# A causal triangular solve with tokens on partitions: 32 tokens in two steps, no transposes between them

## The reference, cut to what matters

```
probs = softmax(q k^T * scale + causal_mask)          # 512 x 512 per head
L     = eye - tril(probs, -1)
rhs   = diagonal(probs)[:, None] * v
A     = solve_triangular(L, rhs, lower=True)          # each token needs all earlier ones
x     = x + A @ Wd.T + bd
```

## Time and profile before

| | |
|---|---|
| median of 3 runs | 1506.54 us (1501.0 to 1509.91) |
| profiled execution, span | 1507.1 us (0.6 us over the median) |
| the layer of the change | about 628 to 1181 us; its 16 solves 719 to 1181 us |
| PE busy | 1237.4 us (82%), 11642 matmuls |
| PEld busy | 673.8 us (45%), 11642 weight loads |
| DVE / ACT / POOL busy | 1035.0 / 729.2 / 628.0 us |
| instruction blocks fetched by DMA queue q8 | 92, 1.51 MB |

### The profile page before, as it was taken

One profiled execution on the slowest core, in us unless ns is written; L12 is line 12 of the kernel. 1 busy time (PEld: TensorE's weight loads), 2 busy tenths in 40 slices (PEclk: granted clock), 3 DMA queues, 4 the chain that ended last, 5 costly groups with the idle time before them and its releaser, 6 DMA issues. The chain is left out here.

```text
span 1507.1 us, 30851 instructions
## 1 busy us (share of the span) xinstructions
PE 1237.4 (82%) x11642; PEld 673.8 (45%) x11642; DVE 1035.0 (69%) x2290; ACT 729.2 (48%) x1596; POOL 628.0 (42%) x838
## 2 busy tenths in 40 slices
PE   6656677779999988538889988988988799999976
PEld 2212232222333337424666766666666333333276
DVE  6699999979888955457446646645632588988653
ACT  3834334317766675313524523533442166676754
POOL 2279888853424215314423423223332524351244
PEclk9878888869999998758889879978997599999988
DMA  5378833023224022441421231141120231331213
GB/s 166 145 274 320 298 139 140 20 67 87 55 65 122 13 82 63 100 86 23 88 38 25 45 74 28 21 100 18 18 51 10 67 79 31 97 89 45 81 48 88
DMA packets 137737, 128.41 MB, mean 85 GB/s; under 512 B 92007, under 2 KB 123559, under 8 KB 132202
## 3 DMA queue, kind: packets, MB, share of 16 engines
q1 hardware_dynamic: 129536, 118.56, 28.6%
q0 software_dynamic: 2496, 5.13, 1.1%
q10 hardware_dynamic: 5558, 2.76, 0.9%
HBM read 105.61 MB, written 38.62 MB: 96 GB/s over the span
## 5 line engine op out<-in xcount | busy, mean ns | idle before, releaser
L1393 DVE TENSOR_REDUCE f_row_min<-f_ps 128x1 f32<-128x512 f32 x512 | 323.9, 676 | 55.6 <-PE f_ps L1720 55.2
L1283 ACT ACTIVATE f_e<-f_ps 128x512 f32<-128x512 f32 x512 | 282.8, 602 | 126.4 <-PE f_ps L1740 122.5
L1720 PE MATMUL f_ps<-f_operands 72*128 72x512 bf16 x512 | 205.4, 410 | 26.4 <-DMA f_operands<-k_scr 15.4
L1740 PE MATMUL f_ps<-f_operands 75*128 75x512 bf16 x512 | 189.5, 380 | 2.6 <-ACT f_e L1283 2.1
L790 PE MATMUL m_ps<-m_shared,sb_ident 128*128 128x512 f32 x256 | 136.8, 683 | 58.1 <-DVE m_shared L630 58.0
L363 POOL TENSOR_TENSOR m_drive<-m_du,m_ring 128x1024 f32<-128x1024 f32 x64 | 149.7, 2352 | 56.2 <-DVE m_ps L622 37.6
L495 ACT ACTIVATE m_ps<-m_delta,m_A 128x511 f32<-128x511 f32 x128 | 83.0, 681 | 131.7 <-DVE m_ps L622 109.0
L1751 PE MATMUL f_ps<-f_e,f_v_op 128*32 128x512 f32 x1024 | 136.4, 604 | 2.1 <-ACT f_e L1283 1.4
L2714 DVE TENSOR_TENSOR d_aT<-d_ps,d_aT 128x16 f32<-128x16 f32 x224 | 37.9, 169 | 140.9 <-PE d_ps L2892 140.7
L1720 PEld LDWEIGHTS f_ps<-f_operands 72*128 72x128 bf16 x512 | 51.3, 101 | 181.2 <-DVE f_row_min L1393 127.3
L2545 DVE TENSOR_REDUCE d_row_min<-d_ps 128x1 f32<-128x384 f32 (+3 forms) x176 | 106.3, 634 | 35.9 <-PE d_ps L2786 34.7
(11 more groups left out here) (298 smaller groups left out, 2345.3 us busy)
## 6 DMA issues: line engine op xcount, KB each, us to landing
m_ring<-bc_scr SPq DMA_DIRECT2D x32, 1024.0 KB, 5.4
f_rows_scr<-blank SPq DMA_DIRECT2D x2, 8707.5 KB, 30.8
f_wall<-f_wall SPq DMA_DIRECT2D x16, 578.0 KB
f_operands<-q_scr SPq DMA_DIRECT2D x32, 288.0 KB
f_operands<-k_scr SPq DMA_DIRECT2D x96, 96.0 KB
d_q_op<-q_scr SPq DMA_DIRECT2D x6, 576.0 KB
d_k_op<-k_scr SPq DMA_DIRECT2D x18, 192.0 KB
f_operands<-f_rows_scr SPq DMA_DIRECT2D x46, 64.5 KB, 1.8
```

The lines of the kernel that those rows point to most:

```text
L1283: nc.scalar.activation(e_sb[:, n % 3, hh, :], ps[:, SCORE[(b * UNITS + u) % SCORE_BANKS], :], ACT.Exp, scale=SCALE).then_inc(s["e_out"], 1)
L1393: nc.vector.tensor_reduce(row_min[:, b % 2, u // TPB, u % TPB:u % TPB + 1], ps[:, MAXQ[(b * UNITS + u) % MAX_BANKS], :], AX.X, ALU.max, ne ...
L1720: nc.tensor.matmul(ps[:, MAXQ[n % MAX_BANKS], :], q_op(b, QK)[:, hd, t * P:(t + 1) * P], k_op(b, QK)[:, hd, :], start=True, stop=True).the ...
L1740: nc.tensor.matmul(ps[:, SCORE[n % SCORE_BANKS], :], k_op(b, QKS)[:, hd, t * P:(t + 1) * P], q_op(b, QKS)[:, hd, :], start=True, stop=True ...
```

## The change

Tokens stay on partitions. A tile is four windows of 32 tokens; each window is solved in two steps (`j` = 0 to 7, window `j // 2`), and every step computes all 32 tokens of its window, for all 16 heads, into one PSUM bank: 4 column groups of 32 partitions, head `i * 4 + hh` in group `hh`, columns `i * 8` on. The weights are now 32 columns of `xT` or `mT`, and the moving side is 8 channels. `own_part` multiplies by `xT` and starts the bank; `known_part` adds `mT` times the tokens solved so far; VectorE copies the window into `a_all` in four copies (one for each column group), from which both the next step and later tiles read. So that the second step of a window can compute the first half again, GpSimd clears the diagonal blocks of the first halves in `e_nat` before `mT` is made. Two banks alternate between steps, one accumulates the earlier tiles, VectorE's work beside gets three banks instead of two, and ScalarE's keeps two. All transposes of the steps, `gT`, `a_nat` and ScalarE's copies of the solve go; one transpose of the finished tile (`turn_out`, hook 0 of the next) feeds the output projection (hook 2). The wait of SP's load of `xT` for tile `n` is now for all steps of tile `n-2`, not for its first products.

```diff
-TURNS = BLKS - 1
-PADDED = NH * HEAD_COLS + 2 * HD
-HOOKS = 2 * TURNS
+WINDOW = 2 * BLK
+WINDOWS = P // WINDOW
+OUTPUT_AT = 2
+GAPS = ((0,), (1, 2), (3,), (4, 5), (6, 7), (8, 9), (10,), (11,), (12, 13))
+HOOKS = 14
-        STEP, TURN, TO_ACT, TO_DVE = (0, 1), (2, 3), (4, 5), (6, 7)
+        EARLIER, FOLD, TO_ACT, TO_DVE = 0, (1, 2), (3, 4), (5, 6, 7)
+                def clear_first_blocks(n):
+                    pool.wait_ge(s["sums_out"], GROUPS * (n + 1))
+                    pool.wait_ge(s["blk_step"], BLK_STEPS * (n + 1))
+                    for k in range(WINDOWS):
+                        own = slice(k * WINDOW, k * WINDOW + BLK)
+                        nc.gpsimd.memset(e_nat[own, n % 3, :, own], 0.0).then_inc(s["e_cleared"], 1)
...
                     if n >= 2:
-                        sp.wait_ge(s["at_ps"], 2 * BLKS * (n - 2) + 2)
+                        sp.wait_ge(s["step_ps"], BLKS * (n - 1))
...
+                def leave_window(n, j):
+                    dve.wait_ge(s["step_ps"], BLKS * n + j + 1)
+                    for hh in range(GROUP):
+                        last = nc.vector.tensor_copy(solved(n, j, hh), left_by(j, hh))
+                    last.then_inc(s["window_out"], 1)
...
+                    if n >= 0 and n % TPB:
+                        with_earlier(n)
+                    for gap, hooks in enumerate(GAPS):
+                        if n >= 0 and gap >= 1:
+                            leave_window(n, gap - 1)
+                        for h in hooks:
+                            beside(n, h)
...
+                def earlier_tiles(n, tiles):
+                    t = n % TPB
+                    for j in tiles:
+                        for hd in range(NH):
+                            for k in range(WINDOWS):
+                                last = nc.tensor.matmul(of_head(ps[window(k), EARLIER, 0:H], hd), e_off[t][:, hd, j, window(k)],
+                                                        of_head(a_all[:, j, :], hd), start=(j == 0 and hd == 0), stop=(j == t - 1 and hd == NH - 1))
...
+                def own_part(n, j):
...
+                    for i in range(GROUPS):
+                        for hh in range(GROUP):
+                            hd = i * GROUP + hh
+                            last = nc.tensor.matmul(of_head(folded(j, hh), i), xT[rows, n % 2, hd, window(k)], of_head(g[rows, :], hd),
+                                                    start=(i == 0), stop=(j == 0 and i == GROUPS - 1))
...
+                def known_part(n, j):
...
+                    pe.wait_ge(s["window_out"], BLKS * n + j)
...
+                            last = nc.tensor.matmul(of_head(folded(j, hh), i), mT[rows, n % 2, hd, window(k)],
+                                                    of_head(a_all[rows, n % TPB, :], hd), start=False, stop=(i == GROUPS - 1))
...
+                    if n >= 0 and n % TPB:
+                        from_earlier(n)
+                    for gap, hooks in enumerate(GAPS):
+                        if n >= 0 and gap == 1:
+                            own_part(n, 0)
+                        if n >= 0 and gap >= 2:
+                            known_part(n, gap - 1)
+                        if n >= 0 and 1 <= gap < BLKS:
+                            own_part(n, gap)
+                        for h in hooks:
+                            beside(n, h)
```

More of the change, by code:

```diff
@@ L2663, in beside @@
                         values(b)
-                    if begins_early(n + 1) and h == 13:
-                        first_tiles(n + 1)
                     b = goes_on(n, 4)
@@ L2885, in beside @@
                         project(goes_on(n, 5), h)
-                def side_by_side(half, lhs, rhs, rows, cols, done):
-                    for gl in range(2):
-                        for hh in range(GROUP):
-                            hd = head(half, gl, hh)
-                            last = nc.tensor.matmul(ps[hh * HEAD_COLS:(hh + 1) * HEAD_COLS, STEP[half], cols],
-                                                    of_head(lhs[rows, :], hd), rhs(hd), start=(gl == 0), stop=(gl == 1))
-                    last.then_inc(done, 1)
@@ L2896, in turn_half @@
-                def turn_half(half, src, done):
-                    nc.tensor.transpose(turn_bank(half), src[:, half, :], core.ident[:, :]).then_inc(done, 1)
-                def output(n):
-                    bank = dve_free("output", n)
-                    for half in range(2):
-                        last = nc.tensor.matmul(bank[:, 0:P], aT[:, n % 2, half, :], w["d_wd"][:, half, :],
-                                                start=(half == 0), stop=(half == 1))
-                    last.then_inc(s["dve_ps"], 1)
@@ L2906, in earlier_tiles, with turn_out @@
-                def earlier_tiles(n, half, out, tiles):
-                    t = n % TPB
-                    for gl in range(2):
-                        for j in tiles:
-                            for hh in range(GROUP):
-                                hd = head(half, gl, hh)
-                                last = nc.tensor.matmul(out[hh * HEAD_COLS:(hh + 1) * HEAD_COLS, :],
-                                                        of_head(a_all[:, j, :], hd), e_off[t][:, hd, j, :],
-                                                        start=(gl == 0 and j == tiles[0]), stop=(gl == 1 and j == tiles[-1]))
+                def turn_out(n):
+                    pe.wait_ge(s["window_out"], BLKS * (n + 1))
+                    nc.tensor.transpose(act_free("aT", n)[:, 0:P], a_all[:, n % TPB, :], core.ident[:, :]).then_inc(s["act_ps"], 1)
@@ L2915, in earlier_tiles @@
                     return last
                 def first_tiles(n):
-                    bank = dve_free("first_tiles", n)
-                    for half in range(2):
-                        last = earlier_tiles(n, half, bank[:, half * P:(half + 1) * P], range(n % TPB - 1))
-                    last.then_inc(s["dve_ps"], 1)
-                def from_earlier(n, half):
-                    t = n % TPB
-                    pe.wait_ge(s["an_sb"], 2 * BLKS * n - 1 + half)
-                    earlier_tiles(n, half, step_bank(half), range(t - 1, t)).then_inc(s["g_ps"], 1)
@@ L2928, in inverse @@
-                def inverse(n, half):
-                    pe.wait_ge(s["gn_sb"], 2 * n + half + 1)
-                    side_by_side(half, g_nat[:, :], lambda hd: xT[:, n % 2, hd, :], slice(0, P), slice(0, P), s["at_ps"])
-                def product(n, half, k):
-                    pe.wait_ge(s["an_sb"], 2 * (n * BLKS + k - 1) + half + 1)
-                    own = slice(k * BLK, (k + 1) * BLK)
-                    rows = slice(0, k * BLK)
-                    side_by_side(half, a_nat[:, :], lambda hd: mT[rows, n % 2, hd, own], rows, own, s["at_ps"])
@@ L2962, in _ @@
[L2962 to L2973 removed]
+                        pe.wait_ge(s["zero_set"], 1)
```

225 lines of the change are left out of this document (81 added, 144 removed).

## The result

The changed kernel takes 1570.45 us (median of 4 runs, 1566.61 to 1572.75), the kernel before 1508.02 beside it (4 runs, 1501.0 to 1509.91). The ratio is 1.0424, 95% interval 1.0395 to 1.0452: 62 us slower. Forecast were 1499.5, faster.

The account below looks back on a forecast made before the run. TensorE was taken to pace 45% of a batch, SP's queue walks the rest. From 1507.1 us, -32 for TensorE and +25 for instruction fetch gave 1500 us (1499.5 against the median), own range 1488 to 1511, overall 1468 to 1527.

Parts of the forecast that it names:

- -32 for TensorE: Solve: 15% saved where TensorE paces, -25 us over three batches, and -7 in the last 47 us; 1475 us.
- +25 for the fetch: TensorE's dense stretches: instruction blocks at 3.75 us per 256 instructions give back 25 us of the saving.
- Pairs: own_part and known_part: 32-column, 8-moving-column pairs follow at 8.7 ns, so 32 pairs cost 0.39 us.
- rival 3: Solve's 8-column pairs: a floor of 26 ns each, no faster than 128-column ones; +45, 1552 us; chance 6%.
- Blocks: TensorE's instruction queue: some 43 more blocks on q8, 3.75 us per 256 instructions in a dense stretch.
- Rival 2: 384-pair runs and last three tiles: blocks cost more, 4.25 us each; +13, 1520 us, slower; chance 22%.
- The averaging over a tile: Tile before a t = 3 start: 7.75 blocks take 29.1 us against 29.7, leaving 0.6 of 4.6 us saving.
- Rival 1: Instruction fetch doesn't bind, so the whole -32 stays: 1475 us, as low as 1462; chance 25%.
- A step's latency: Solve step with nothing beside it: 1.1 us, of which four VectorE copies 0.5 (0.42 to 0.74).
- rival 4: Lock-step: copies queue behind VectorE's reductions, gaps wait for hooks, the saving goes into waits; 1507 us; chance 9%.
- GpSimd's clearing: Four memsets after the inversion, before mT: cost nothing, or delay mT by at most their own 2 us.
- SyncE's walks: SP's queue, three walks a batch without solve steps: stay at 17.8, 19.8 and 30.7 us within 2 us.

Follow-up runs that it names:

- experiment 4: The kernel before, with each product with an earlier tile cut from one matmul of 128 moving columns into four of 32 (2304 pairs more): 1560.7 us, ratio 1.0348.
- experiment 5: The changed kernel, with the earlier tiles multiplied as before (2304 pairs fewer) and the new solve steps kept: 1536.14 us, ratio 1.0178.
- experiment 7: The changed kernel, with earlier tiles multiplied as before and own part computed once per window: 1528.25 us, ratio 1.0138.
- experiment 10: The best form: changed kernel, earlier tiles multiplied as before, own part once per window, two of four copies on ScalarE in first steps: 1516.44 us, ratio 1.0068.
- experiment 8: Two of a step's four copies on ScalarE: in the changed kernel 1567.85 us; with earlier tiles multiplied as before, from 1536.14 to 1529.37 us.
- experiment 11: The changed kernel without GpSimd's clearing for 15 of 16 heads: 1572.08 us, ratio 1.0447.
- Experiment 9: The version of experiment 7 plus 96 unread bf16 matmuls of 512 columns, in front of known_part of steps 1 to 6: 1533.18 us, ratio 1.0183.
- experiment 1: The changed kernel, with the earlier tiles' part multiplied with 128 columns of weights at once instead of four times 32: 1632.61 us, ratio 1.0835.
- experiment 6: The changed kernel plus 192 unread bf16 matmuls of 384 columns between the 8-column ones of the earlier tiles' part: 1590.5 us, ratio 1.0545.

## Why the prediction was wrong

Its sum was -32 for TensorE, +25 for the fetch. Point by point:

- *Pairs.* 32 pairs follow in 0.26 to 0.27 us from first to last start at full clock (median), 8.5 ns each against 8.7 forecast. Right; rival 3 is out. The floor of about 25 ns that the prediction takes from the Trainium skill ("TensorE: Matmul & The Clock Gate") stands there in the section "Wait — 56ns, not 53.3ns?"; the 8.5 ns disagree with it.
- *Blocks.* 44 more, forecast 43. The rate of 3.75 us in a dense run was about right too (3.8 us in the middle of 11, 3.45 to 4.57). Rival 2 is right in its sign. Its mechanism, a block above 4.0 us because other transfers share the DMA engines, holds for the three long stops where the next batch is loaded: the blocks there began late, by some 9 us in all. Elsewhere 5 of the 11 blocks took over 4.0 us, at most 4.57.
- *The averaging over a tile*: this step failed. "992 pairs, 1984 instructions, 7.75 blocks: 29.1 us against 29.7" supposes that fetch time unused in one place is there in another. It isn't. The stretch from one tile's first `own_part` to that of the `t` = 3 tile (the first row) lasted 44.0 us, with 1022 pairs recorded:

```profile
930.10:974.07 43.97, 37.00 (x1022) 28.50 (x1021) 25.54 (x83) 9.45 (x19) 13.14 (x37) 0.63 0.16 25
1199.59:1226.18 26.59, 20.43 (x900) 18.48 (x899) 6.55 (x34) 2.61 (x5) 0.00 (x0) 0.63 0.07 10
1226.18:1241.90 15.72, 10.77 (x486) 9.12 (x485) 6.33 (x34) 0.53 (x2) 0.00 (x0) 0.50 0.02 5
```

  While TensorE works through mT and scores, 16 instructions in 1 to 2 us, hardly more than a block gets ahead: a block on q8 began at 958.54, and the run at 958.58 came to its first stop after 132 pairs, 264 instructions. The 384 pairs at the start need three blocks in a row, and each that isn't there costs 3.5 to 4.6 us less the 1.3 it takes to run; the two stops of this run are 1.56 and 3.31 us. They are 4.9 of the 5.5 us of stops in that stretch. The rest of the 14 us over the 29.7 of before is work, of more pairs at a lower clock: 37.0 us busy at 0.63, against 25.4 at 1.00. Where a whole stretch is dense, the number held: forecast 26.7 us for the tile before the last and 14.2 for the last, measured 26.6 and 15.7 (the second and third row), with blocks on q8 3.7 us apart on average. But only 8 of those 42 us are stops, and the clock of 0.63 and 0.50 wasn't in the forecast, so the match is in part luck. The term was put at 25 us and is 54 of stops. Experiments 4 and 5 show that the instructions do it: +53 by adding them alone, -34 by taking them out of the earlier tiles' products.
- *The clock* had no term at all. The earlier trace rows showed 0.72 and 0.77 in the tiles where TensorE waits most, and the prediction used them only as an argument for rival 2. No price was worked out from them. By the count above this is 29 us, and it stayed when the stops had gone (experiments 7 and 10); why it stayed no run shows by itself. Of the 22 falls of the clock in the changed kernel's solves, nine came within 3.4 us of a run of the earlier tiles' products with a stop in it; the others behind steps, mT with waits, or idle stretches.
- *The saving of 32.* In the best form, with the stops back at the level of before, the solve is 9.5 us longer with 36 more at half clock, so by this estimate 26 us of saving are there and paid away, after 27 us more of waits for VectorE, ScalarE and DMA. Rival 1's 1475, no fetch and so all the saving, is refuted with it: without the stops it's 1516 to 1528.
- *A step's latency.* 1.51 us against 1.1, at half clock: four copies take 0.78, not 0.5, because each lasts its full 186 ns, with nothing saved from one to the next; my upper bound was 0.74. In the changed kernel that cost nothing that experiment 8 could tell. Once the instructions had been reduced, a faster first step gave 12 us (experiment 10 against 7). So rival 4's waits were real but hidden behind the supply.
- *GpSimd's clearing:* nothing that can be told from noise, as forecast (experiment 11).
- *SyncE's walks:* 20.9, 22.0 and 31.4 us against 17.8, 19.8 and 30.7. Two grew by more than the 2 us that the prediction allowed, so they aren't as free of TensorE as it read them: scores, maxima and turns stand inside them, and TensorE was slower there. VectorE's idle time before the inverted sums, the prediction's sign that the walks hold, fell from 21.9 to 18.1 us. A batch grew from 123.8 to 146.5 us, 6 of it in the walks and 17 in the rest. SyncE's queue, the walk from the stores of `e`:

```profile
923.78 5.20 SPq L2275 DMA_DIRECT2D e_scr<-d_e_nat  x8
...
933.97 5.05 SPq L2299 DMA_DIRECT2D d_xT<-x_scr  x8
939.07 0.45 SPq L2283 DMA_DIRECT2D z_scr<-d_zT  x1
```

What stays open: the clock was moved only together with other things. Of the 20 us that are left without stops, 12 went with a faster first step (experiment 10). For the last 10 there are two candidates, which no run separates: the half clock (36 us by the count), and TensorE's waits for the other engines and DMA (27 us more than before). VectorE's load could be at most 8 of them. Experiment 9 moved clock and price together but not the time, and no run raised the clock alone, so its share, 29 us in the changed kernel too, is counted from medians, not shown. Over 58 runs of the kernel before, whose mean clock lay between 0.878 and 0.894, a clock lower by 0.01 went with 4.2 us more (95% about 1.8 to 6.6); 0.04 lower would be 17. That agrees, but either may cause the other.

The Trainium skill ("Runtime: NRT & Kernel Launch", Instruction fetch mechanics) gives TensorE room for 2048 instructions. By it the 768 instructions of a start would have been ahead after the sparse hooks; the stop of 1.56 us that begins at 959.87, after 132 pairs or 264 instructions, disagrees. The measurement decides.

## What to carry to other kernels

Before an engine's work is cut into many short instructions, count the instructions of each dense run in blocks of 256, not the mean of a phase: here a block that wasn't ahead took 3.5 to 4.6 us, whatever the array needed, stops of 5 to 7 us stood where a batch was being loaded, and idle fetch time elsewhere didn't pay for it. Price TensorE's work at the clock that the new mix will have: here the new steps ran at a granted clock of 0.73 to 0.76, the old at 0.87, and the large matmuls beside them with them. And a step that is made faster was worth nothing while the stream that carries it was late.

## What the runs showed of the hardware that was not expected

- Pairs with 128 columns of weights and 8 moving columns start 112 ns apart at full clock and 213 at half (medians, experiment 1), hardly less than with 128 moving columns (eight pairs in 1.16 and 2.02 us at the two levels). Four pairs of 32 columns in four column groups take 35 ns together at full clock.
- 17 of 18 stops of TensorE over 1 us end 1.3 to 1.65 us after a block of instructions has arrived. While a batch is loaded the block comes late: in the stop of 7.2 us before 1035.98 it began on q8 only after 4.3 us, with the DMA engines busy for 77%.
- Half clock is not a state of idleness: 24 us of unbroken work ran at it (928.3 to 952.3).
- Four copies of 32 elements a partition from PSUM take 0.78 us on VectorE (186 ns each) and 178 ns each on ScalarE.
- A bf16 matmul of 384 columns put between 8-column pairs takes 0.27 us at full clock from its start to the next pair's (median, experiment 6), where 0.16 had been put.
